# Five of 762 gathers of the second kind, copied row by row from SyncE's queue

## What the reference computes

```python
msgs = z[edge_dst] @ Wd + z[edge_src] @ Ws + edge_weight[:, None] * ww[None, :] + bm
agg = jax.ops.segment_max(msgs, edge_dst, num_segments=n)
agg = jnp.where(deg[:, None] > 0, agg, 0)
hidden = relu(z @ W1a + agg @ W1b + b1);  x = layernorm(x + hidden @ W2 + b2)
# second layer, twice:  mean = segment_sum(x[src], dst) / max(deg, 1);  mean @ Wl.T + bl + x @ Wr.T
x = layernorm(x + out)
```

## Time and profile before

| | |
|---|---|
| Time, median of 3 runs | 1208.82 us (1207.52 to 1213.25) |
| The profiled execution's own time | 1212.43 us |
| Its span in the profile | 1210.6 us |
| Busy: PE, PEld, DVE, ACT, POOL | 1097.6, 811.8, 854.4, 368.9, 752.1 us |
| Mean granted TensorE clock | 0.82 |
| First gather of zs_d begins, last one ends | 42.3 us, 1011.6 us |

### The profile page before, as it was taken

The page is one execution under the profiler, slowest core; times in us unless marked ns, Lnnn a source line. Parts: engine busy times, 40 slices in busy tenths (PEclk is TensorE's granted clock), DMA queues, the critical chain, the costliest instruction groups (busy, mean ns, idle before and its releaser), DMA issues. The chain is left out here.

```text
span 1210.6 us, 23225 instructions
## 1 busy us (share of the span) xinstructions
PE 1097.6 (91%) x6896; PEld 811.8 (67%) x6927; DVE 854.4 (71%) x3110; ACT 368.9 (30%) x1189; POOL 752.1 (62%) x789
## 2 busy tenths in 40 slices
PE   5799998998899888999899798988999988899998
PEld 5477777776677666777667676667766666565554
DVE  6466787777776778778786778777787878365444
ACT  3223333333332333333333333333333323131000
POOL 4766777777777777777777777777777773000000
PEclk9657687767776788658895889987698999999999
DMA  7323333333333333343343344333444353452110
GB/s 193 103 66 80 83 101 93 86 103 91 93 87 106 88 105 87 92 99 108 99 94 87 93 126 106 86 93 87 119 116 104 89 152 91 134 158 59 31 31 24
DMA packets 116573, 116.33 MB, mean 96 GB/s; under 512 B 23330, under 2 KB 101625, under 8 KB 116441
## 3 DMA queue, kind: packets, MB, share of 16 engines
q1 hardware_dynamic: 89356, 62.25, 18.7%
q0 software_dynamic: 25024, 51.30, 16.7%
q10 hardware_dynamic: 2061, 1.20, 0.4%
HBM read 102.00 MB, written 12.68 MB: 95 GB/s over the span
## 5 line engine op out<-in xcount | busy, mean ns | idle before, releaser
L810 POOL DMA_INDIRECT area<-zs_d,area x762 | 729.0, 957 | 240.6 <-issue 227.7
L980 DVE TENSOR_TENSOR_SCAN area<-area,bank 128x512 f32<-128x512 bf16 x196 | 249.0, 1270 | 234.8 <-PE bank L1313 219.9
L679 ACT CAST adj_w<-bank 128x325 f32 x391 | 175.8, 450 | 624.0 <-PE bank L1373 607.7
L1367 PEld LDWEIGHTS bank<-area 128*128 128x128 f32 x1564 | 266.4, 241 | 35.0 <-ACT area L687 12.3
L1367 PE MATMUL bank<-area 128*128 128x13 f32 x1564 | 271.2, 286 | 12.2 <-issue 8.4
L961 DVE TENSOR_SCALAR area<-area 128x325 bf16<-128x325 f16 x782 | 251.3, 321 | 0.0
L960 DVE TENSOR_SCALAR area<-area 128x128 bf16<-128x128 f16 x782 | 211.5, 270 | 0.0
L1370 PE MATMUL bank<-area 128*128 128x325 bf16 x782 | 210.8, 359 | 0.0
L1313 PE MATMUL bank<-ident,area 128*128 128x128 f32 x762 | 152.6, 333 | 61.4 <-DMA area<-zs_d,area 61.2
L1313 PEld LDWEIGHTS bank<-ident,area 128*128 128x128 f32 x762 | 97.4, 164 | 120.9 <-DMA area<-zs_d,area 84.3
L1354 PE MATMUL bank<-ident,area 128*128 128x128 f32 x782 | 161.0, 342 | 0.0
(11 more groups left out here) (159 smaller groups left out, 844.5 us busy)
## 6 DMA issues: line engine op xcount, KB each, us to landing
area<-mask_d SPq DMA_DIRECT2D x195, 128.0 KB
area<-zs_d,area POOLq DMA_INDIRECT x762
area<-wp_d SPq DMA_DIRECT2D x585, 3.0 KB
area<-parts_d SPq DMA_DIRECT2D x20, 384.0 KB, 7.6
zr_d<-area SPq DMA_DIRECT2D x24, 128.0 KB
area<-zr_d SPq DMA_DIRECT2D x6, 512.0 KB, 3.9
parts_d<-area SPq DMA_DIRECT2D x23, 96.0 KB
adj_w<-in_x_dram SPq DMA_DIRECT2D x3, 512.0 KB, 5.4
```

Source lines behind the costliest of these rows:

```text
L679: nc.scalar.copy(adj[:, :, bass.ds(at, W)], A_BANK[s % 2][:, 0:COLS].rearrange("p (h w) -> p h w", w=W))
L810: pool.indirect_dma_start(gring[:, g % GR * 4 + s % 2 * 2 + u, :], None, x if g < RAW else zs_d[0:N, :], bass.IndirectOffsetOnAxis(ap=src_ ...
L980: nc.vector.tensor_tensor_scan(S[:, g % 2, 0:n], mask[:, g % MR, 0:n], T_BANK[g % 2][:, 0:n], S[:, (g + 1) % 2, 511:512] if g else 0.0, AL ...
L1367: nc.tensor.matmul(o[:, 384:384 + W], St[:, b * P:(b + 1) * P], sel[:, g % 2, u, s % 2, :], start=u == 0, stop=u == 1)
```

## The change

The groups 38, 70, 102, 134 and 166 (`OWN`: every 32nd from 38) get their fourth block of 128 rows another way. GpSimd issues three gathers for each of them instead of four. SP copies the 128 rows itself, one DMA of 512 bytes a row, from zs_d into `own` (the last 256 words of `raw_w`, two buffers of 128 rows). It does so over the 32 slots before the group's own: in each of the slots 6 to 165 it loads four node numbers from SBUF into registers, in one call, and issues four copies with a register in the source's address. The 128 node numbers of a group come as one DMA into partition 96 of `edge`, two slots before the group's first rows. PE waits for the 128 copies with a semaphore of their own (`l_own`) before the fourth transpose of such a group, and its counts for `landed` allow for the missing gathers. SP also waits once, before its loop, until zs_d is written (`zs_st`).

```diff
+ROWS = 4
+STEP = -(-P // ROWS)
+OWN = tuple(range(STEP + 6, NG - 2, STEP))
+def landings(g):
+    return sum(4 - (i in OWN) for i in range(g % GR, g + 1, GR))
+        own = raw_w[:, 6 * F:8 * F].rearrange("p (a f) -> p a f", f=F)
+        own_r = edge[96:97].bitcast(i32)
+        l_own_r, l_own = sem("l_own_r"), [sem(f"l_own{i}") for i in range(2)]
@@ sync
+                nodes = []
+
+                def own_rows(k):
+                    for i, g in enumerate(OWN):
+                        at = (4 * g + 3) * P
+                        if k == g - STEP - 2:
+                            if i >= 2:
+                                sp.wait_ge(t_ps, OWN[i - 2] + 1)
+                            sp.dma_start(own_r[:, i % 2, 0:P], src[at:at + P].rearrange("(o e) -> o e", o=1)).then_inc(l_own_r, 16)
+                        for r in range(max(0, (k - g + STEP) * ROWS), min(P, (k - g + STEP + 1) * ROWS)):
+                            if r == 0:
+                                sp.wait_ge(l_own_r, 16 * (i + 1))
+                            if r % ROWS == 0:
+                                nodes[:] = nc.values_load_multi_w_load_instructions(
+                                    own_r[:, i % 2, r:r + ROWS], engines=[mybir.EngineType.SP], min_val=0, max_val=N - 1,
+                                    skip_runtime_bounds_check_because=NODES)[1]
+                            sp.dma_start(own[r:r + 1, i % 2, :], zs_d[bass.ds(nodes[r % ROWS], 1), :]).then_inc(l_own[i % 2], 16)
+
                 sp.wait_ge(wp_st, 16 * (BB - 1))
+                sp.wait_ge(zs_st, 16 * NX)
                 for k in range(NG + 5):
                     if 2 <= k < NG:
                         load_edges(k)
+                    own_rows(k)
@@ gpsimd
-                    for u in range(2):
+                    for u in range(1 if g in OWN and s % 2 else 2):
@@ tensor
-                pe.wait_ge(landed[g % GR], 64 * (g // GR) + 64)
+                pe.wait_ge(landed[g % GR], 16 * landings(g))
...
-                    pe.wait_ge(landed[g % GR], 64 * (g // GR) + 16 * (n // P))
+                    pe.wait_ge(landed[g % GR], 16 * (landings(g) - 4 + n // P))
                     for b in range(n // P):
-                        last = nc.tensor.matmul(o[:, b * P:(b + 1) * P], gring[:, g % GR * 4 + b, :], ident[:, :],
+                        rows = gring[:, g % GR * 4 + b, :]
+                        if g in OWN and b == 3:
+                            i = OWN.index(g)
+                            pe.wait_ge(l_own[i % 2], 16 * P * (i // 2 + 1))
+                            rows = own[:, i % 2, :]
+                        last = nc.tensor.matmul(o[:, b * P:(b + 1) * P], rows, ident[:, :],
```

More of the change, by code:

```diff
@@ L36 @@
 LATE = NT - 3
+ROWS = 4
+STEP = -(-P // ROWS)
+OWN = tuple(range(STEP + 6, NG - 2, STEP))
 MERGED = 22 * P
 ORDER = (5, 0, 1, 2, 3, 4, 6)
+NODES = "a source node, which is below N"
 STARTS = "a superbatch's first destination node, which is below N"
```

## The result

The changed kernel takes 1201.97 us (median of 20 runs, 1197.76 to 1210.57), the kernel before beside it 1207.66 us (20 runs, 1204.87 to 1216.54). The ratio is 0.9953, 95% interval 0.9934 to 0.9972: 0.47% or 5.7 us less. The forecast was 0.52% less. Every ratio here is the one on record with its interval. One run in all counts as slow, an execution of 1228.83 us with six rows and one weight load, and is left out of its ratio.

A forecast was written before the change was run, and what follows sets the result against it. POOL's end-to-end gathers were taken to bound the loop: five fewer at 1.262 us save 6.3 us, 1212.43 to 1206.1, scaled to the 1208.82 median as 1202.5 us (0.52% less). Range for 8 in 10: 1199 to 1214 us.

The forecast's parts named there:

- POOL paces, PE only looks busy: Main loop: POOL runs gathers end to end, 1.262 us each; PE, 91% busy, still waits 61.2 us for them.
- Five gathers are 6.3 us and all of it arrives: POOL's loop after 110.8 us: 5 x 1.262 = 6.3 us less; PE follows, so the whole gain reaches the end.
- SP's new work: SP, slots 6 to 165: one four-value register load plus four address calculations and DMAs, 2.56 us a slot (2.1 to 4.3).
- What is to spare: SP's waits for scans over slots 6 to 165: 535.1 / 160 = 3.34 us a slot, 0.8 us left after the new work.
- The turning point: SP's cost per copied row at which SP starts to pace: 0.575 us, against the 0.38 taken.
- The rival's formula: SP as pacer: time = 1208.8 + 160 x (c - 3.34), c being SP's new work in us a slot.
- The short slots: SP's queue in a 2.99 us slot: next mask load 1.8 us late, near 308.5; weight loads still land in time.
- PE's reserve: PE's waits for landed gathers over the loop, about 60 us, from which small delays by late loads would come.
- PE's new wait: PE's wait for a group's last four copied rows: about 5.9 us of cover, gone only if SP lags over a slot.
- The gain is eaten: Rival, chance 0.20: c near 3 us uses up PE's reserve, PE sets the loop's length; about 1208.8 us, no change.
- SP becomes the pacer: Rival, chance 0.18: SP's new work exceeds 3.34 us a slot, so SP sets slot length; 1250 us at 3.6, 1362 at 4.3.

The follow-up runs named there:

- POOL's part alone: Changed kernel without SP's row copies and PE's wait for them; five gathers left out, part of the maximum not computed: ratio 0.9944 to the kernel before.
- SP's part alone: Changed kernel, but POOL gathers all 762 blocks and PE transposes the gathered ones; SP's copies are made but not used: ratio 0.9983 to the kernel before.
- second measurement: Changed kernel with an extra one-value register load a slot, which was not in the program that ran: ratio 0.9945 to the kernel before.

## Why the prediction held, step by step

- *POOL paces, PE only looks busy.* Shown, by forty gathers left out: 50.9 us for 50.5 by count times pitch, at an unchanged pitch of 1.261 us.
- *Five gathers are 6.3 us and all of it arrives.* Shown within what the runs can tell: 0.9944 for POOL's part alone, 0.9953 for the whole change, 0.9948 forecast. That the forecast's 1202.5 us lies 0.5 us from the median has luck in it: it was scaled from the median of three executions of a kernel whose executions spread by 12 us. What the mechanism says is the difference, 5.7 us measured for 6.3.
- *SP's new work.* Hidden, as forecast, but mis-sized: 2.56 us a slot was the sum, 2.85 is what one slot measures, 2.90 the mean and 3.00 what SP's waits lost by it. The load of four registers took 1.12 us for 1.0, and the copies are 0.43 us apart ((1.52 - 0.232) / 3) for 0.38, mostly the move of 29 ns and its gap; the DMA was cheaper, 0.232 for 0.26, although a register is in its source. At 0.43 us a row copy stays under the 0.57 that would have made the prediction wrong.
- *What is to spare.* 3.34 us a slot, from the waits of before, and so 0.8 us left. Left were 0.35 us of waits for scans, which is 3.34 less the 3.00 that the work took in all. The prediction counted the instructions but neither the slower issues beside them nor the gap behind the last. The turning point given, 0.575 us a row at four rows, was not tried as such; that SP paces beyond 3.34 us a slot was, with 3.45 us, at a loss of 29 us. The rival's formula gives 20 us for it (25 with the 3.48 of the one slot read). With six rows and one weight load, 3.27 us a slot already cost 8 us, where the formula gives nothing: it is too sharp at the edge.
- *The short slots.* SP came late, and somewhat more than worked out: the next mask load of the earlier trace rows was put near 308.5, and 308.32 is the time in the new trace, but its slot began at 303.21 instead of 303.77. From mask load to mask load it is 5.11 us for the 4.75 forecast; the two errors nearly cancel. I put the price to PE at "a few tenths here and there"; it was 22.3 us of waits for weight loads. They came out of PE's reserve, so its waits for gathers were 38.6 us instead of the 55 forecast, and the time did not move.
- *PE's new wait.* None in the trace.
- *The rivals.* "The gain is eaten" was nearer than the result shows: with 22.3 of 61 us of reserve taken and 0.35 us a slot left on SP, one row a slot more tips it; that case's own condition, PE setting the loop's length, did not come about. "SP becomes the pacer" is what that one row brings. The Trainium skill's floor of about 600 ns for a register load (DMA: Bandwidth & Descriptors, section Latency and other measured facts) does not hold for each value: four came in 1.12 us with one instruction. Nor is it a floor here for one instruction, since a load of one register took 464 ns.

## What to carry to other kernels

Here the engine with constant short rests between equal instructions paced, at 62% busy, and not the one at 91%; count times pitch then gave what leaving some out is worth. Look for the same pattern before trusting busy shares. Work put on another queue was free up to the wait that this queue had per turn of the loop. The trace of before gave that limit to about 0.1 us a turn, if the work is counted with its gaps and with what it slows, and over many turns: one turn read from a timeline can be long or short. Near the limit the cost sets in a little early; beyond it every turn pays. A new wait in the trace is a cost only if the old one behind it has not shrunk by as much.

## What the runs showed of the hardware

Executions of one kernel fall into two clusters 7 to 8 us apart. The gap is plainest with one weight load and five rows, where no execution lies between 1196.6 and 1203.7 us; in the two kernels of the main comparison it is narrow. The 20 of the changed kernel lie at 1197.8 to 1203.5 (12 of them) and 1205.7 to 1210.6; those of before spread likewise, 1204.9 to 1208.8 and 1210.2 to 1216.5. Two traces show where: the windows view from 45 to 110 us, first of the kernel before (profiled execution 1212.43 us), then of SP's part alone (1203.54 us), with busy times of PE, PEld, DVE, ACT, POOL, granted clock, DMA share, GB/s.

```profile
45.00:110.00 65.00, 63.04 (x278) 45.96 (x278) 36.66 (x144) 18.64 (x58) 43.59 (x46) 0.53 0.31 78
```

```profile
45.00:110.00 65.00, 57.10 (x356) 42.63 (x356) 46.76 (x180) 22.74 (x73) 49.44 (x52) 0.79 0.36 87
```

At a granted clock of 0.53, nearly all 1.2 GHz, PE got through 278 matmuls in this stretch, at 0.79 through 356. POOL is held up by the ring of four groups in the first case, and since POOL paces what follows, these waits are not made up: the last gather starts at 1010.6 us in the first trace and at 1002.2 in the second. POOL's waits for PE over the span, in the same two traces (sum, times, longest):

```profile
POOL area L810 <- PE bank L1313: 12.8, 15, 5.8
```

```profile
POOL area L841 <- PE bank L1348: 3.7, 12, 0.3
```

The difference is 9.1 us, somewhat more than what lies between the clusters; between 45 and 110 us alone it is 8.6 us against none. The two kernels differ, but the other traces agree: the five profiled executions of the upper cluster beside the first (the changed kernel in two runs, POOL's part alone, one weight load with four and with five rows) have a clock of 0.51 to 0.53 in this stretch and 13.3 to 15.9 us of such waits. What makes the clock rise early in one execution and not in another was not tried.

Sorted by cluster, the differences are steadier than the medians, which depend on how many executions fell where. In the main comparison 12 of 20 fell in the lower cluster for either kernel, so its medians compare like with like. Medians of each cluster, and what they are below those of the kernel before in the same cluster:

| | lower | upper |
|---|---|---|
| Changed kernel (20) | 1199.64 against 1206.38: 6.7 us less | 1207.46 against 1213.48: 6.0 us less |
| The same, second measurement (12) | 1197.55 against 1204.95: 7.4 | 1206.58 against 1213.40: 6.8 |
| One weight load, four rows (12) | 1200.72 against 1206.62: 5.9 | 1208.62 against 1214.03: 5.4 |
| One weight load, five rows (12) | 1196.50 against 1204.47: 8.0 | 1204.63 against 1213.13: 8.5 |

The changed kernel's four figures lie around the 6.3 of five gathers, and those of the last row near the 8.8 of seven. That speaks for the last being the better kernel by 1 to 2 us. It is not shown: two measurements of one program differ by nearly as much, and the intervals overlap.
